# A gated cross-attention and expert block on one core: values with batch and group innermost, x's first load in two, the half tile's products by what they wait for, and a new order

## The reference, cut to what matters

```python
# x: (8, 256, 256)   ctx: (8, 77, 192)   16 heads of 16
def xattn(x, y):
    q, k, v = x @ wq + bq, y @ wk + bk, y @ wv + bv       # split in heads
    attn = softmax(q @ k.T / sqrt(16))                    # per batch and head
    return (attn @ v) @ wo + bo
def ffn(x):                                               # 2048 tokens, 256 -> 1024 -> 256
    top1 = argmax(softmax(x @ gate_w.T))                  # one of two experts
    masked = x[None] * one_hot(top1).T[:, :, None]
    routed = sum over e of relu(masked[e] @ w1[e] + b1[e]) @ w2[e] + b2[e]
    return routed + relu(x @ sw1 + sb1) @ sw2 + sb2
x = x + tanh(g_xattn) * xattn(layernorm(x), ctx)
x = x + tanh(g_ffn) * ffn(layernorm(x))
```

## Time and profile before

| | us |
|---|---|
| median of 3 runs | 338.06 |
| lowest and highest | 336.54, 340.1 |
| profiled execution | 337.8 |
| its span in the trace | 336.0 |

### The profile page before, as it was taken

How to read it: one execution, slowest core, us unless ns; L and a number is a source line. 1 busy time by engine, 2 the same in 40 slices (tenths; PEclk the granted TensorE clock), 3 DMA queues, 4 the chain that set the end, 5 groups by cost and what they waited for, 6 DMA issues and landing times.

```text
span 336.0 us, 7284 instructions
## 1 busy us (share of the span) xinstructions
PE 315.3 (94%) x2383; PEld 282.6 (84%) x2383; DVE 225.8 (67%) x516; ACT 214.4 (64%) x483; POOL 185.7 (55%) x264
## 2 busy tenths in 40 slices
...
GB/s 140 270 236 53 264 30 19 73 135 25 7 19 2 16 160 0 2 1 67 0 2 5 198 266 66 126 32 189 2 217 209 56 172 94 70 26 94 94 31 28
DMA packets 31780, 29.37 MB, mean 87 GB/s; under 512 B 16398, under 2 KB 28690, under 8 KB 31243
## 3 DMA queue, kind: packets, MB, share of 16 engines
...
## 4 chain that ended last, share of the span: by engine, by line
PE 72%; DVE 6%; POOL 5%; issue 3%; ACT 3%; ACTq 0%; DVEq 0%; POOLq 0%
PE y_ps L1540 25%; PE h_ps L1540 19%; PE s_ps L1540 10%; PE bank L1540 9%; PE bank L1679 4%; PE bank L1715 1%; PE bank L1782 1%; POOL probs L686 1%; POOL nt L727 1%; DVE smax L1252 1%; DVE probs L1264 1%; DVE rsum L1270 1%; DVE h L1511 1%; ACT probs L950 1%; DVE hT_lo L1518 1%
## 5 line engine op out<-in xcount | busy, mean ns | idle before, releaser
L1540 PE MATMUL y_ps<-sw,hT_hi 128*128 128x256 f32 x272 | 57.0, 292 | 0.9 <-DVE hT_lo L1518 0.6
L1474 DVE TENSOR_TENSOR hT_lo<-h,hT_hi 128x256 fp32r<-128x256 f32 x64 | 29.9, 467 | 37.2 <-ACT h L1091 37.2
L1540 PE MATMUL y_ps<-ew,hT_hi 128*128 128x256 f32 x256 | 52.9, 285 | 0.0
L686 POOL TENSOR_TENSOR probs<-probs,rinv 128x616 f32<-128x616 f32 x32 | 39.4, 1246 | 22.6 <-DVE rinv L1273 22.4
L1540 PEld LDWEIGHTS y_ps<-sw,hT_hi 128*128 128x128 f32 x272 | 44.7, 191 | 2.8 <-DVE hT_lo L1518 1.9
L1540 PE MATMUL h_ps<-x2T_hi,sw 128*128 128x512 f32 (+1 forms) x160 | 43.8, 361 | 0.0
L1540 PEld LDWEIGHTS y_ps<-ew,hT_hi 128*128 128x128 f32 x256 | 42.3, 189 | 0.1
L1540 PE MATMUL y_ps<-sw,hT_lo 128*128 128x256 f32 x136 | 38.4, 282 | 0.0
L1540 PE MATMUL y_ps<-ew,hT_lo 128*128 128x256 f32 x128 | 36.0, 281 | 0.0
L1000 ACT ACTIVATE hT_hi<-h_ps,vec_cols 128x512 fp32r<-128x512 f32 (+1 forms) x40 | 24.4, 610 | 17.6 <-PE h_ps L1540 13.1
L960 ACT ACTIVATE pT<-bank 128x512 f32<-128x512 f32 x40 | 23.8, 606 | 18.4 <-PE bank L1679 18.1
(11 more groups left out here) (208 smaller groups left out, 825.1 us busy)
## 6 DMA issues: line engine op xcount, KB each, us to landing
...
x_all<-in_x SPq DMA_DIRECT2D x1, 1536.0 KB, 7.0
...
```

The source lines that it names most:

```text
L686: nc.gpsimd.tensor_tensor(pq, pq, inverse, ALU.mult).then_inc(p_ready, 1)
L1474: nc.vector.tensor_tensor(hT[1][:, c % HB, 0:RTOK], h32[:, c % 2, 0:RTOK], hT[0][:, c % HB, 0:RTOK], ALU.subtract).then_inc(h_lo, 1)
L1540: return nc.tensor.matmul(out_, lhsT, rhs, start=start, stop=stop, **kw)
```

## The change

Four edits. The values are kept with batch and group innermost (`v32`, `v_pair`, `v_left`), so that a transfer within SBUF has runs of 512 bytes in place of 64; for that the value product writes its columns in another order, `value_rows` evicts in two operations, and `attend` reads its weights with a step of 8 elements. The first load of x is cut in two: the first tile on SyncE's queue, the second on ScalarE's, ahead of the context. In the half tile TensorE waits for the rounded part before two of three products and for the low part only before the third; in its last chunk VectorE makes the full hidden row in ScalarE's place, and GpSimd's addition waits for the last low part. And all five tables are new. A line or two of them:

```diff
 PE_ORDER = """
...
-    y.4.1 y.4.2 y.4.3 h.4.6 h.4.7 y.4.4 y.4.5 y.4.6 y.4.7 xst.1
...
+    y.4.0 y.4.1 h.4.4 h.4.5 y.4.2 h.4.6 y.4.3 h.4.7 y.4.4 y.4.5 xst.1 y.4.6 y.4.7
 SP_ORDER = """
-    kw.0 kw.1 kr.1 kr.2 wd.0 wd.1 vr.0 kr.3 kr.4 fl.0 wd.3 vr.1 kr.5 kr.6 kr.7 wd.2 wd.4 wd.5 ps.0 ps.1 ps.2 xs ps.3
+    kw.0 kw.1 kr.1 vr.0 wd.0 wd.1 kr.2 kr.3 kr.4 fl.0 vr.1 kr.5 wd.3 kr.6 wd.2 ps.0 kr.7 wd.4 wd.5 ps.1 ps.2 ps.3 xs
...
@@ -249,8 +249,8 @@
         wqo_sb = [sb(f"wqo_{n}", [P, 2, KC, DIM], F32R, scope=att) for n in ("hi", "lo")]
-        v_pair = sb("v_pair", [P, 2, BATCHES, GROUPS * HP, PD], scope=att)
-        v_left = sb("v_left", [P, BATCHES, GROUPS, P], scope=att)
+        v_pair = sb("v_pair", [P, 2, 2, HP, PD, VALUE_BATCHES * GROUPS], scope=att)
+        v_left = sb("v_left", [P, 2, P, VALUE_BATCHES * GROUPS], scope=att)
         probs = sb("probs", [P, 2, 4, GK], scope=att)
@@ -282,7 +282,8 @@
         qT = stage[:, 1, GROUPS * GK:GROUPS * GK + GROUPS * SEQ].rearrange("p (g s) -> p g s", g=GROUPS)
-        v32 = [held[0:KEYS, :, :].rearrange("k a c -> k (a c)").rearrange("k (m b d) -> k m b d", m=2, b=VALUE_BATCHES)
+        v32 = [held[0:KEYS, :, :].rearrange("k a c -> k (a c)").rearrange(
+            "k (q x f n) -> k q x f n", q=2, x=2 * HP, f=HEAD_DIM)
                for held in (v_first, h32)]
@@ -412,6 +413,7 @@
         half_sum = sem("half_sum")
+        half_hi = sem("half_hi")
         half_32 = sem("half_32")
@@ -448,7 +450,7 @@
         def _(sp):
-            sp.dma_start(x_all[:, 0:TB, :], x_rows[:, 0:TB, :]).then_inc(x_in[0], 16)
+            sp.dma_start(x_all[:, 0:1, :], x_rows[:, 0:1, :]).then_inc(x_in[0], 16)
             at = 0
@@ -485,24 +487,23 @@
-                batches = slice(share * VALUE_BATCHES, (share + 1) * VALUE_BATCHES)
                 sp.wait_ge(cleared[1], 3 * (share + 1))
                     rows = KEYS if half == parity else split
-                    heads = v32[share][key:key + rows, half, :, :].rearrange("k b (c q f) -> k (b c) q f", q=2, f=HEAD_DIM)
-                    cols = slice(parity * HEAD_DIM, (parity + 1) * HEAD_DIM)
-                    sp.dma_start(v_pair[to:to + rows, half, batches, :, cols].rearrange("p b c f -> p (b c) f"),
-                                 heads[:, :, parity, :]).then_inc(v_in[share], 16)
+                    head = slice(parity * HEAD_DIM, (parity + 1) * HEAD_DIM)
+                    sp.dma_start(v_pair[to:to + rows, half, share, :, head, :].rearrange("p i f n -> p i (f n)"),
+                                 v32[share][key:key + rows, parity, half * HP:(half + 1) * HP, :, :].rearrange(
+                                     "k i f n -> k i (f n)")).then_inc(v_in[share], 16)
                 for half in range(2):
                     key = split if half == 0 else 0
-                    left = v32[share][key:key + LEFT, half, :, :].rearrange("k b (g d) -> k (b g) d", g=GROUPS)
                     for i in range(HP):
-                        first = (2 * i + 1 - half) * HEAD_DIM
+                        first = half * HR + (2 * i + 1 - half) * HEAD_DIM
                         rows = slice(half * HP * LEFT + i, (half + 1) * HP * LEFT, HP)
-                        sp.dma_start(v_left[rows, batches, :, half * HR + first:half * HR + first + HEAD_DIM].rearrange(
-                                     "p b g f -> p (b g) f"), left[:, :, first:first + HEAD_DIM]).then_inc(v_in[share], 16)
+                        sp.dma_start(v_left[rows, share, first:first + HEAD_DIM, :].rearrange("p f n -> p (f n)"),
+                                     v32[share][key:key + LEFT, 1 - half, half * HP + i, :, :].rearrange("k f n -> k (f n)")
+                                     ).then_inc(v_in[share], 16)
@@ -608,10 +609,9 @@
-                batches = slice(share * VALUE_BATCHES, (share + 1) * VALUE_BATCHES)
                 for half in range(2):
-                    nc.gpsimd.memset(v_pair[:, half, batches, :, :], 0.0).then_inc(cleared[1], 1)
-                nc.gpsimd.memset(v_left[:, batches, :, :], 0.0).then_inc(cleared[1], 1)
+                    nc.gpsimd.memset(v_pair[:, half, share, :, :, :], 0.0).then_inc(cleared[1], 1)
+                nc.gpsimd.memset(v_left[:, share, :, :], 0.0).then_inc(cleared[1], 1)
@@ -834,6 +834,7 @@
             pool.wait_ge(half_in, 16 * 2)
+            pool.wait_ge(half_lo, HC)
             nc.gpsimd.tensor_tensor(half_part[:, :], half_part[:, :], half_other[:, :], ALU.add).then_inc(half_added, 1)
@@ -845,6 +846,7 @@
         def _(act):
+            act.dma_start(x_all[:, 1:TB, :], x_rows[:, 1:TB, :]).then_inc(x_in[0], 16)
             act.dma_start(y_sb, ctx_768.rearrange("b s d -> s b d")).then_inc(context_in, 16)
@@ -887,9 +889,12 @@
                 at = 2 * j % VALUE_BATCHES
-                nc.scalar.activation(v32[2 * j // VALUE_BATCHES][:, :, at:at + 2, :].rearrange("k m n d -> k n m d"),
-                                     value_bank(j).rearrange("k (n m d) -> k n m d", n=2, m=2), ACT.Copy
-                                     ).then_inc(v_32, 1)
+                own = slice(at * GROUPS, (at + 2) * GROUPS)
+                for q in range(2):
+                    ins = nc.scalar.activation(
+                        v32[2 * j // VALUE_BATCHES][:, q, :, :, own].rearrange("k x f n -> k x n f"),
+                        value_bank(j).rearrange("k (x n q f) -> k x n q f", x=2 * HP, n=2 * GROUPS, q=2)[:, :, :, q, :], ACT.Copy)
+                ins.then_inc(v_32, 1)
@@ -1110,7 +1115,9 @@
                 nc.scalar.activation(hT[0][:, c % HB, 0:P], h32[:, c % 2, 0:P],
-                                     ACT.Relu, bias=half_b1[:, c:c + 1])
+                                     ACT.Relu, bias=half_b1[:, c:c + 1]).then_inc(half_hi, 1)
+                if c == HC - 1:
+                    continue
                 if c >= 2:
@@ -1146,7 +1153,7 @@
-                dve.wait_ge(x_in[min(b, 2)], 16)
+                dve.wait_ge(x_in[min(b, 2)], 32 if b == 0 else 16)
                 tiles = range(b * TB, (b + 1) * TB)
@@ -1515,6 +1522,7 @@
                 dve.wait_ge(half_32, c + 1)
+                dve.wait_ge(half_hi, c + 1)
                 nc.vector.tensor_tensor(hT[1][:, c % HB, 0:P], h32[:, c % 2, P:2 * P], hT[0][:, c % HB, 0:P],
@@ -1526,7 +1534,12 @@
                 half_hidden_lo(c - 1)
-            half_hidden_lo(HC - 1)
+            c = HC - 1
+            dve.wait_ge(half_in, 16 * 2)
+            dve.wait_ge(half_sum, HC)
+            nc.vector.tensor_scalar(h32[:, c % 2, P:2 * P], h32[:, c % 2, 0:P], half_b1[:, c:c + 1], 0.0, ALU.add, ALU.max
+                                    ).then_inc(half_32, 1)
+            half_hidden_lo(c)
             dve.wait_ge(half_y, HC)
@@ -1598,8 +1611,8 @@
                         b, rows = 2 * j + n, slice(0, CK + 1 if k == 0 else CK)
-                        ins = mm(value_bank(j)[:, n * DIM:(n + 1) * DIM], yT[rows, k, b * KEYS:(b + 1) * KEYS],
-                                 wv_sb[rows, k, :].rearrange("p (g m d) -> p m g d", g=GROUPS, m=2), k == 0,
+                        ins = mm(value_bank(j).rearrange("k (x n d) -> k x n d", x=2 * HP, n=2)[:, :, n, :], yT[rows, k, b * KEYS:(b + 1) * KEYS],
+                                 wv_sb[rows, k, :].rearrange("p (g x d) -> p x g d", g=GROUPS, x=2 * HP), k == 0,
                                  k == CKC - 1)
@@ -1688,10 +1701,10 @@
                         cols = slice(i * PD, (i + 1) * PD)
-                        mm(bank[m][cols, g * SEQ:(g + 1) * SEQ], v_pair[:, i // HP, b, g * HP + i % HP, :],
+                        mm(bank[m][cols, g * SEQ:(g + 1) * SEQ], v_pair[:, i // HP, b // VALUE_BATCHES, i % HP, :, b % VALUE_BATCHES * GROUPS + g],
                            pT[:, g * CHUNKS + i, :], g == 0, False, skip_group_check=True)
                 for g in range(GROUPS):
-                    ins = mm(bank[m][:, g * SEQ:(g + 1) * SEQ], v_left[0:ROWS[PAIRS], b, g, :],
+                    ins = mm(bank[m][:, g * SEQ:(g + 1) * SEQ], v_left[0:ROWS[PAIRS], b // VALUE_BATCHES, :, b % VALUE_BATCHES * GROUPS + g],
                              pT[0:ROWS[PAIRS], g * CHUNKS + PAIRS, :], False, True, skip_group_check=True)
@@ -1885,12 +1898,15 @@
                     c = n - HALF_LAG
-                    pe.wait_ge(half_lo, c + 1)
+                    pe.wait_ge(half_hi, c + 1)
                     if c == 0:
                         pe.wait_ge(final_rdy, rounds)
-                    ins = cut(y_ps[:, 0, :], lambda m: hT[m][:, c % HB, 0:P], lambda m: sw2_sb[m][:, c, :], c == 0,
-                              c == HC - 1, skip_group_check=True)
-                    ins.then_inc(half_y, 1)
+                    for m in range(2):
+                        mm(y_ps[:, 0, :], hT[0][:, c % HB, 0:P], sw2_sb[m][:, c, :], c == 0 and m == 0, False,
+                           skip_group_check=True)
+                    pe.wait_ge(half_lo, c + 1)
+                    mm(y_ps[:, 0, :], hT[1][:, c % HB, 0:P], sw2_sb[0][:, c, :], False, c == HC - 1,
```

(12 more changed lines are left out.)

81 lines of the change are left out of this document (35 added, 46 removed).

## The result

The changed kernel takes 334.95 us (median of 14 runs, 332.89 to 336.75) against 338.07 for the kernel before: a ratio of 0.9921, with 0.9892 to 0.9949 as its 95% interval. It gains 3.1 us, where 7.0 were forecast. The profiled execution took 336.75 us, of which 334.9 are span; it is among the two longest of the 14.

A forecast was written before the change was run, and what follows sets the result against it. TensorE was busy 315.3 of 336.0 us, with VectorE full at 20 to 50 and 60 to 80. Terms -2.4 - 1.7 + 0.4 - 2.4 - 1.2 - 0.5 + 0.8 = -7.0 from 337.8 gave 330.8, stated as 331.0; range 327.0 to 336.6.

The forecast's parts named there:

- The values' transfers: SyncE's issue of a values share ahead of batch 2's keys: 5.6 us instead of 14.8, hidden, with 1.7 us slack.
- Start: VectorE's first microseconds: root steps run ahead of the keys, statistics begin at 19.1, first maximum at 25.4; 2.4 us won.
- Product of batch 0: Attention near 50 us: value products ahead of batch 2's third score fill TensorE's wait; 1.7 us won, bounds 0 and 2.35.
- Strided reads: Value weights read 32 bytes apart: surcharge of 8-byte reads (0.5 ns a column), a tenth unhidden, 0.4 us lost.
- Seam and clock: Between shared and routed half, near 222 us: shorter hole wins 2.4 us, less low clock behind it 1.2.
- Tail: Last chunk: VectorE makes the full hidden row, last sum at about 331.0; 0.5 us won, bounds 0 and 0.9.
- The sign I gave for it: For the tail: the last sum comes under 1.6 us after the last low part begins.
- New waits: Plan steps delaying the shared half's low parts, and holes from any new order: 0.8 us lost, bounds 0 and 3.
- (b): Rival: attention stays bound by VectorE, start and hole at 50 pay nothing, clock falls as before; 336.3 us, chance 0.14.
- (a): Rival: the start gives nothing, since the context lands as much later as the small steps win; 333.4 us, chance 0.13.
- (e): Rival: values' issue time doesn't fall with the descriptors, 7.5 us of delay against 7.0 won; 338.6 us, chance 0.04.

The follow-up runs named there:

- keys first: The changed kernel with batch 2's keys issued ahead of the first share of the values: 329.67 us, ratio 0.9769 to the kernel before.
- the second experiment: The changed kernel with batch 2's keys still behind the values' share, but ahead of the two 1 MB weight loads: 330.8 us, ratio 0.9783.
- product late: As keys first, with batch 0's products with the values behind batch 2's third score again: 332.85 us, ratio 0.9819.
- the old order: The kernel before with nothing but the new layout of the values; order, start, seam and tail unchanged: 338.56 us, ratio 1.0031.
- seam late: As keys first, with the plan's steps and the turning of the sorted rows back in their places in the kernel before: 334.94 us, ratio 0.9916.

## Why the prediction was wrong, step by step

**The values' transfers: "hidden", with 1.7 us of slack. This step failed.** The chain allows a comparison leg by leg. Batch 1's keys began at 22.80, not 19.5 (+3.3). They took 6.06 us for 5.8 (+0.3), the values 6.90 for 5.6 (+1.3), the weights 1.06 for 1. Batch 2's keys landed 10.0 us after their first issue, and not 7.8 (+2.2). Together 46.85 instead of 39.7, where 42.4 was wanted (46.99 - 4.62). I had put all the doubt on the issue time, of which I took 5.6 where 6.7 was measured, and had none for the two landings. The price is 5.3 us (keys first).

The last leg is shown: those keys landed behind 2 MB of weights. The first is only read from profiles: the keys' write, issued 2.7 us earlier than before (15.06 for 17.74), landed 1.4 us later. Issued close behind x's 1.5 MB it took 7.7 us, against 3.6 before; in the second experiment, issued at 18.21, it took 5.1. No run moved x or the write alone, so the cause of this leg stays open.

**Start, -2.4:** 1.1 at the first maximum (27.80 to 26.67). Its parts were small: 0.6 for the order of the steps, nothing for the transfer; the rest is not separated. The statistics of batches 2 to 7 began at 20.52 and not 19.1, because the root's steps, counted at 0.16 us, were partly as long as the 0.78 shown above (four of them, 3.2 us in all). The trace of before had five such steps, 0.64 to 1.21 us long, between 14.3 and 20.4; I had read only a short one.

**Product of batch 0, -1.7:** the idea was right, the size too small, 3.2 (product late). In the changed kernel it could not show, since batch 2's keys held up everything ahead of it; the products came at 53.15.

**Strided reads, +0.4:** 1.05 in the old order, which the times can't tell from 0.4, and up to 1.8 by the products' rows, 0.23 a batch where I had 0.05; by these rows "a tenth of the surcharge" was too low. The loads of 128 columns became 134 ns longer (331 against 197), twice the 8-byte surcharge of some 64, and of 32 columns 29 ns (144 against 115). The Trainium skill, page "SBUF — State Buffer", section "Door 1: The DMA port swizzle", has each access to a new line of 16 bytes cost something; the 331 ns agree with that in direction.

**Seam and clock, -2.4 and -1.2:** 5.3 together by the medians, and 3.2 and 2.3 in the traces (seam late), both near the good end of their bounds. Of the 1.92 us ahead of the turned rows only 0.38 were left, where I had 1.7 exposed, and the clock did not fall, which I had left open.

**Tail, -0.5:** 0.1 to 0.2. The sign I gave for it, a last sum under 1.6 us after the last low part begins, could not tell: it is 1.39 now (329.02 to 330.41) and was 1.35 before (330.15 to 331.50).

**New waits, +0.8:** with the measured terms 338.07 - 1.1 - 3.2 + 1.05 - 5.3 - 0.2 = 329.3, and keys first has 329.67, which leaves 0.4 for them. Its trace has one such wait that the kernel before lacks, 0.81 us at 234.49 (0.92 at 241.60 in the changed kernel). These terms come from different bases and from medians that are each uncertain by 1.0 to 1.7 us, so the sum closes no better than that. Adding the 5.3 us of the late keys gives 334.95 by construction, since they are the difference of the two medians.

Of the rivals, (b) with 336.3 came nearest in time, hardly nearer than (a) with 333.4, and by luck: VectorE had a hole instead of being the bound. (e) had the right mechanism, a late load of batch 2's keys, at an issue time that had fallen; I had tied the delay to the issue time alone.
